# Attention inside a fused kernel: value sums for two batches in one product, the next x transposed ahead of the head products, and the key product in a bank of its own

## The reference

```python
q, k, v = split_heads(layernorm(x) @ w_qkv.T)
dots = q @ k.T                                  # per head, no softmax
attn = dots / max(norm(dots), EPS) * norm_g + norm_b
x = x + layernorm(merge_heads(attn @ v) @ w_out.T + b_out)
x = x + layernorm(soft_moe(layernorm(x)))       # 8 experts, 128 slots each
```

## Time and profile before

| what | value |
|---|---|
| median of 3 runs | 839.48 us |
| the three runs | 839.48, 839.47, 840.86 us |
| the profiled execution, its own time | 840.9 us |
| its span, first to last instruction | 839.1 us |
| mean granted TensorE clock | 0.998 |
| TensorE busy | 831.7 us, 99% |
| VectorE busy | 643.9 us, 77% |
| ScalarE busy | 549.1 us, 65% |

### The profile page before, as it was taken

The page is one execution under the profiler, slowest core; times in us unless marked ns, Lnnn a source line. Parts: engine busy times, 40 slices in busy tenths (PEclk is TensorE's granted clock), DMA queues, the critical chain, the costliest instruction groups (busy, mean ns, idle before and its releaser), DMA issues.

```text
span 839.1 us, 15012 instructions
## 1 busy us (share of the span) xinstructions
PE 831.7 (99%) x4890; PEld 723.0 (86%) x4890; DVE 643.9 (77%) x1296; ACT 549.1 (65%) x1078; POOL 86.3 (10%) x103
## 2 busy tenths in 40 slices
PE   9999999999999999999999999999999999999997
PEld 8988999887888888888988888888888888899997
DVE  8788888899899989998866666666666665477776
ACT  5666767567787887789546555555555554567775
POOL 0200000043223333450000000000000000000000
PEclk9999999999999999999999999999999999999999
DMA  7011121202323252125020303011020303066883
GB/s 246 21 51 51 50 75 39 63 26 77 106 97 124 89 201 98 67 96 207 1 100 1 101 1 100 0 65 35 16 84 0 100 0 101 1 203 215 286 289 112
DMA packets 52561, 75.37 MB, mean 90 GB/s; under 512 B 3104, under 2 KB 33696, under 8 KB 52384
## 3 DMA queue, kind: packets, MB, share of 16 engines
q1 hardware_dynamic: 52512, 74.76, 26.8%
HBM read 49.59 MB, written 25.17 MB: 89 GB/s over the span
## 4 chain that ended last, share of the span: by engine, by line
PE 93%; DVE 4%; ACT 1%; issue 1%; DMA 0%; DVEq 0%; POOL 0%; ACTq 0%; POOLq 0%
PE bank L996 21%; PE bank L1026 13%; PE bank L1068 11%; PE bank L865 9%; PE bank L890 9%; PE bank L1029 7%; PE bank L785 3%; PE bank L874 3%; PE bank L735 3%; PE bank L684 2%; PE bank L768 2%; PE bank L758 1%; PE bank L746 1%; PE bank L1004 1%; PE bank L716 1%; PE bank L705 1%
## 5 line engine op out<-in xcount | busy, mean ns | idle before, releaser
L996 PE MATMUL bank<-snT,w_r 128*128 128x512 f32 x768 | 194.8, 393 | 0.0
L1471 ACT ACTIVATE act<-bank,b_sb 128x512 f32<-128x512 f32 x128 | 88.0, 687 | 139.3 <-PE bank L996 138.9
L2085 DVE TENSOR_TENSOR act_r<-act,act_r 128x512 fp32r<-128x512 f32 x128 | 88.2, 690 | 111.0 <-ACT act_r L1476 110.8
L1026 PE MATMUL bank<-w_r,act_r 128*128 128x512 f32 x480 | 173.2, 397 | 0.0
L996 PEld LDWEIGHTS bank<-snT,w_r 128*128 128x128 f32 x768 | 136.6, 188 | 28.7 <-issue 0.3
L1029 PE MATMUL bank<-w_r,act_r 128*128 128x256 f32 x480 | 134.6, 280 | 0.0
L1026 PEld LDWEIGHTS bank<-w_r,act_r 128*128 128x128 f32 x480 | 90.2, 188 | 21.0
L890 PE MATMUL bank<-disp_r,y_r 128*128 128x512 f32 x384 | 103.5, 406 | 0.4 <-DVE disp_r L1938 0.3
L865 PE MATMUL bank<-yT_r,snT 128*128 128x512 f32 x384 | 99.4, 395 | 0.0
L1029 PEld LDWEIGHTS bank<-w_r,act_r 128*128 128x128 f32 x480 | 90.7, 189 | 4.1
L1068 PE MATMUL bank<-eo_r,comb_r 128*128 128x258 f32 x768 | 92.3, 283 | 0.0
(11 more groups left out here) (203 smaller groups left out, 1321.3 us busy)
## 6 DMA issues: line engine op xcount, KB each, us to landing
combine_scratch<-comb SPq DMA_DIRECT2D x64, 256.0 KB, 2.0
stage<-in_w SPq DMA_DIRECT2D x16, 1024.0 KB, 6.5
stage<-combine_scratch SPq DMA_DIRECT2D x4, 2048.0 KB, 9.1
snT<-combine_scratch SPq DMA_DIRECT2D x4, 2048.0 KB, 9.5
x_scratch<-stage SPq DMA_DIRECT2D x8, 512.0 KB, 3.2
x<-x_scratch SPq DMA_DIRECT2D x8, 512.0 KB, 4.0
x_d<-x_scratch SPq DMA_DIRECT2D x8, 512.0 KB, 9.6
slots_eo<-in_x SPq DMA_DIRECT2D x7, 512.0 KB, 4.4
```

Of the source, the lines that this page charges most:

```text
L996: last = pe.matmul(hidden_bank(e, i)[:, :], w1_r[q][:, a, k, j * P:(j + 1) * P], sl_r[f][:, c, k, :], start=(n == 0), stop=(n == len(steps ...
L1026: pe.matmul(bank[BH + c][:, :].rearrange("p (w d) -> p w d", w=2), act_r[:, i % RING, 0, c * S:(c + 1) * S], w2_r[q][:, :, j, :], start=(j ...
L1471: act_fn(act[:, i % 2, :], hidden_bank(e, i)[:, :], ACT.Gelu, bias=b1_sb[:, ds(e * KH + i % KH, 1)])\
L2085: v.tensor_tensor(act_r[:, i % RING, 1, :], act[:, i % 2, :], act_r[:, i % RING, 0, :].bitcast(F32), ALU.subtract).then_inc(h_split, 1)
```

## The change

- `value_sums` is issued in batches 0 and 1 for one batch each, and then in each odd batch for that batch and the one before. `xsum` has two rows for this, and the product has two columns. It stands behind the queries (in batch 0 it stays where it was), and goes into bank 0. VectorE's product with b_col moves out of `keep_heads` into `keep_sums`, which stands ahead of `rest_of_gk` in odd batches, with a semaphore `vb_kept`.
- `transpose_xn(b + 1)` stands between `transpose_o(b-1)` and `head_products(b)`. ScalarE's and VectorE's work on it (`round_xnT`, `rest_of_xnT`) moves from the start of the next batch to the end of this one, on VectorE ahead of `keep_proj`, and after batches 1 and 2 ahead of the slots.
- The key product goes into bank 3 and waits for VectorE's clamp of the norms there.
- The loop runs over pairs of batches.

```diff
-            xsum = sb("xsum", [P, KD])
+            xsum = sb("xsum", [P, 2, KD])
...
+        def sums_through(b, odd, it):
+
+            if isinstance(b, int):
+                return b + 1 if b < 2 else 2 + (b - 1) // 2
+            return it + 3
...
-                    pe.wait_ge(gk_split, b)
+                    pe.wait_ge(qT_ready, b * KD)
+                    if not odd:
+                        pe.wait_ge(vb_kept, sums_through(b - 1, True, it))
...
-                pe.wait_ge(qT_ready, b * KD + 1)
+                if not is_batch(b, 0):
+                    pe.wait_ge(norm_clamped, b)
...
-                        last = pe.matmul(bank[0][:, m * D:(m + 1) * D], gram_r[:, i, k, m * P:(m + 1) * P],
+                        last = pe.matmul(bank[3][:, m * D:(m + 1) * D], gram_r[:, i, k, m * P:(m + 1) * P],
...
             def value_sums(b):
+
+                pair = slice(b, b + 1) if is_batch(b, 0) or is_batch(b, 1) else slice(0, 2)
+                pe.wait_ge(qT_ready, b * KD + 1)
                 for h in range(KD):
                     for k in range(KD):
-                        last = pe.matmul(bank[3][:, h:h + 1],
-                                         wqkvT[:, k, 2 * D + h * P:2 * D + (h + 1) * P], xsum[:, k:k + 1],
+                        last = pe.matmul(bank[0][:, 2 * h + pair.start:2 * h + pair.stop],
+                                         wqkvT[:, k, 2 * D + h * P:2 * D + (h + 1) * P], xsum[:, pair, k],
...
-                if front:
-                    queries(b)
-                if front:
-                    gram_times_k(b)
+                queries(b)
+                if odd:
+                    value_sums(b)
+                gram_times_k(b)
                 if back:
                     transpose_o(b - 1)
-                if front:
+                if not back:
                     value_sums(b)
-                    if not back:
-                        half_of_xn(1)
-                    head_products(b)
+                    half_of_xn(1)
+                elif not before_y:
+                    transpose_xn(b + 1, False, not odd, it)
+                head_products(b)
...
-            with pe.Fori(3, B - 1) as b:
-                attention(b)
+            with pe.Fori(0, B // 2 - 2) as it:
+                attention(2 * it + 3, True, it)
+                attention(2 * it + 4, False, it)
...
                 if following and back:
                     round_xn(b + 1)
+                    round_xnT(b + 1, not odd, it)
...
-                dve.wait_ge(sums_in_psum, b + 1)
-                v.tensor_tensor(vb[:, ds(b % 2, 1), :].rearrange("p a c -> p (a c)"), bank[3][:, 0:KD], b_col[:],
-                                ALU.mult).then_inc(heads_ready, 1)
+                last.then_inc(heads_ready, 1)
+
+            def keep_sums(b, it=0):
+
+                pair = slice(b, b + 1) if is_batch(b, 0) or is_batch(b, 1) else slice(0, 2)
+                n = pair.stop - pair.start
+                dve.wait_ge(sums_in_psum, sums_through(b, True, it))
+                v.tensor_tensor(vb[:, pair, :], bank[0][:, 0:2 * KD].rearrange("p (h a) -> p a h", a=2)[:, pair, :],
+                                b_col[:].unsqueeze(1).to_broadcast([P, n, KD]), ALU.mult).then_inc(vb_kept, 1)
...
+                if odd:
+                    keep_sums(b, it)
                 if front:
                     rest_of_gk(b)
...
                 if following and back:
                     rest_of_xn(b + 1)
+                    rest_of_xnT(b + 1)
```

More of the change, by code:

```diff
@@ L798, in transpose_slots, with attention @@
                     last.then_inc(seT_in_psum, 1)
-            def attention(b, front=True, back=True, first_back=False, second_back=False, before_y=False):
-                if front:
+            def attention(b, odd, it=0, back=True, first_back=False, second_back=False, before_y=False):
+                if is_batch(b, 0) or is_batch(b, 1):
                     transpose_xn(b, not back)
-                    gram_of_x(b, not back)
+                gram_of_x(b, not back)
                 if back:
@@ L1143, in round_second, with round_xnT @@
                 act_fn(xn_r[:, 0, half:NT], xn[:, half:NT], ACT.Copy).then_inc(xn_hi, 1)
-            def round_xnT(b, first):
-                if not first:
+            def round_xnT(b, odd, it=0):
+                if not is_batch(b, 0):
                     sc.wait_ge(qT_in_psum, b * KD)
-                    sc.wait_ge(sums_in_psum, b)
+                if isinstance(b, int) and b >= 2:
+                    sc.wait_ge(sums_in_psum, sums_through(b - 2 if b < 4 else b - 1, True, 0))
+                elif not isinstance(b, int):
+                    sc.wait_ge(sums_in_psum, it + 3)
                 for k in range(KD):
@@ L1174, in round_gk @@
                 sc.wait_ge(gk_in_psum, b + 1)
-                act_fn(gk_r[:, 0], bank[0][:, :].rearrange("p (k d) -> p k d", k=KD), ACT.Copy).then_inc(gk_hi, 1)
+                act_fn(gk_r[:, 0], bank[3][:, :].rearrange("p (k d) -> p k d", k=KD), ACT.Copy).then_inc(gk_hi, 1)
             def keep_qT(b, h, first):
@@ L1186, in root_norm, with round_oT @@
                 act_fn(nrm[:], nrm[:], ACT.Sqrt, bias=zero_col[:]).then_inc(norm_rooted, 1)
-            def round_oT(b, first):
+            def round_oT(b, first, odd, it=0):
                 if not first:
                     sc.wait_ge(proj_in_psum, b)
+                sc.wait_ge(vb_kept, sums_through(b + 1 if not odd and not first else b, True, it))
                 for h in range(KD):
@@ L1194, in round_oT @@
                     alone(sc)
-                    act_fn(oT_r[:, 0, h, :], bank[4 + h][:, :], ACT.Identity, bias=vb[:, ds(b % 2, 1), h:h + 1]
-                           .rearrange("p a c -> p (a c)")).then_inc(oT_hi, 1)
+                    act_fn(oT_r[:, 0, h, :], bank[4 + h][:, :], ACT.Identity, bias=vb[:, int(odd), h:h + 1])\
+                        .then_inc(oT_hi, 1)
             def square_proj(b, first=False, begin=0, end=NT):
@@ L1241, in mean_out_bias, with attention @@
                     .then_inc(bout_summed, 1)
-            def attention(b, front=True, following=True, back=True, end=True, first_back=False, first_end=False,
-                          before_y=False):
+            def attention(b, odd, it=0, front=True, following=True, back=True, end=True, first_back=False,
+                          first_end=False, before_y=False):
                 if before_y:
                     root_x2(0, B // 2)
-                if front:
-                    round_xnT(b, not back)
+                if is_batch(b, 0) or is_batch(b, 1):
+                    round_xnT(b, odd)
                 if front and not back:
@@ L1287, in attention @@
                 if back:
-                    round_oT(b - 1, first_back)
+                    round_oT(b - 1, first_back, not odd, it)
                 if before_y:
@@ L1835, in attention @@
                 if back:
-                    rest_of_oT(b - 1)
+                    rest_of_oT(b - 1, not odd)
                 if first_back:
@@ L1841, in attention @@
                     dve.wait_ge(consts_loaded, 16 * N_CONSTS)
+                if not back:
+                    keep_sums(b)
                 if front:
@@ L1884, in _ @@
             rest_of_wqkv(0)
[L1885 to L1886 removed]
+            attention(0, False, back=False, end=False)
+            attention(1, True, end=False, first_back=True)
             rest_of_slots(0)
[L1888 removed]
+            attention(2, False, first_end=True)
             rest_of_slots(1)
[L1890 to L1892 removed]
+            with dve.Fori(0, B // 2 - 2) as it:
+                attention(2 * it + 3, True, it)
+                attention(2 * it + 4, False, it)
+            attention(B - 1, True, following=False, before_y=True)
             dve.wait_ge(ident_loaded, 16)
```

49 lines of the change are left out of this document (23 added, 26 removed).

## The result

The changed kernel takes 836.80 us (median of 6 runs, 836.57 to 836.92), against 839.49 for the kernel before (6 runs: 839.47, 839.47, 839.48, 839.50, 840.86, 841.01). The ratio of the means is 0.9962, with a 95% interval of 0.9949 to 0.9975. That is 0.3 to 0.4% faster, clear of the noise. Between the medians it is 2.7 us, where 2.1 was forecast. The runs of before fall into two groups, a lower one at 839.5 and an upper one at 840.9 and 841.0, the runs with a stretch at half clock. In these six runs the changed kernel shows no second group.

A forecast was written before the change was run, and what follows sets the result against it. TensorE, busy 99% at full clock, was taken as the bound. Sums -2.43, batch 3's wait -0.40 and batch 7's lost cover +0.75 make -2.08 us, from the median 839.48 to 837.4 us; range 836.7 to 838.0.

The forecast's parts named there:

- The value sums are work: TensorE's value sums: 0.81 us a group is work, not a hidden wait; three groups fewer give -2.43 us.
- The second column is free: Value sums for two batches in one product: the second column was taken as zero cost, 0.3 us in all at most.
- The lost cover in batch 7: Batch 7 has nothing between o transposes and head products, so TensorE waits for gk_r: +0.75 us.
- The moved transposes: xn transposes (0.79) replace value sums (0.81) ahead of the head products; cover 1.66 instead of 1.68 still suffices for gk_r.
- The Gram and the transposes show no wait: After the move xn is 0.28 us early for the transposes and xn_r 0.58 early for the Gram: no wait.
- The gain is carried through: After the attention no TensorE wait over 0.3 us is on the chain, so the gain reaches the end; contrary rival 0.08.
- The wait in batch 3: TensorE's 0.42 us wait for qGq ahead of batch 3's norm products shrinks, 0.02 to 0.2 left: -0.40 us.
- No row there has a wait: Batch 4 of the loop, read by starts on TensorE: its groups' times were taken to hold no wait.
- Batch 3, the one place where TensorE waits: Claimed batch 3, after outputs, as TensorE's only wait: 0.42 us for VectorE's qGq.
- The half clock: Batch 3's queries at 1.2 GHz behind a wait and narrow norm products cost 1.58 us; rival that it stays, 0.14.
- The rival that batch 7's new wait would bring it: Batch 7's new 0.75 wait, or the one left in batch 3, brings half clock in most runs: 839.0, chance 0.14.
- slower: the clock falls again and again: Narrow sums close behind norm products drop the clock in batches 1, 3, 5, 7: 6.3 us, 843.7; chance 0.04.

The follow-up runs named there:

- `slots_first`: The changed kernel with VectorE's rest of xnT of batch 3 behind the last slots again; 838.03 and 838.08 us in two runs, 839.20 to 839.71 in eight, 841.05 in one.
- `slots_unrolled`: `slots_first` with TensorE's batches 3 to 6 written out; 838.03 and 838.07 us in two runs, 839.41 to 839.68 in nine.
- `before_pairs`: The kernel before with ScalarE and VectorE looping over pairs of batches, so the column of vb is a constant; 838.88 us.
- `vb_by_batch`: The changed kernel with a column of vb for every batch, its address worked out in a register in the loop; 837.88 us.
- `sums_ahead`: The changed kernel with the value sums of batches 1, 3, 5, 7 ahead of the norm products; 839.75 to 839.81 us in three runs, 840.98 to 841.47 in eight.
- `slots_filled`: `slots_unrolled` with five unused 512-column products ahead of batch 3's norm products, where TensorE waits for qGq; 837.98 to 838.14 us in six runs.
- `own_sums`: The changed kernel with one-column value sums for each batch, behind the queries, so three groups more; 839.56 us.

## Why the prediction was right or wrong

**Right, by its own steps.** The value sums are work, 0.81 a group: term -2.43, measured -2.39. The second column is free: 0.80 and 0.81 a group in batches 5 and 7, and 0.80 with one column in batch 1. The group of batch 3 takes 0.91; in `slots_first` and `slots_unrolled`, where TensorE comes to it later, it takes 0.81, so the extra 0.1 is most likely a wait, which no run tests by itself. The lost cover in batch 7: +0.75, measured +0.76, and shown by filling it. The moved transposes keep the head products supplied: no wait for gk_r in batches 1 to 6, and 5.5 us lost when they are moved back, 4.6 of it as this wait. The Gram and the transposes show no wait from batch 4 on; in batch 3 a new one of about 0.2 stands between the Gram and gram times q, which the forecast did not have. The gain is carried through. The wait in batch 3: -0.40 forecast; the outputs lost 0.51 and the norm products' restart 0.01 there, but 0.12 and 0.09 came back as the new wait ahead of gram times q, and 0.1 at the value sums; about -0.2 net.

**Wrong: a wait was taken for work.** The step that failed is the reading of batch 4 by starts, with its end "No row there has a wait". Head products 1.56 and projection 2.94 in the earlier trace rows were taken for plain work, so the sum has nothing for them. They hold a wait of TensorE for VectorE's oT_r, and the runs show 0.66 us for its going. The Gram that was to start 2.94 after the projection starts 2.80 after it. The written-out batch 2 of the kernel before has these rows, which I did not use:

```profile
53.69 1.68 PE L716 MATMUL bank<-wqkv_r,gk_r 128*128 128x256 f32 x12
55.20 2.97 PE L785 MATMUL bank<-wout_r,oT_r 128*128 128x256 f32 x24
58.01 1.03 PE L796 MATMUL bank<-ident,slots_eo 128*128 128x128 f32 x8
```

1.51 and 2.81 for the same instructions. The loop's projections waited for oT_r, in which `vb[:, ds(b % 2, 1)]` had its address worked out in a register on both engines. The loop over pairs turned it into a constant. In batches 3 to 6 the head products and projections give 0.66 us less, which `before_pairs` confirms as 0.6 in the time. That the address is what made oT_r late is shown in two batches of `vb_by_batch`, 0.15 us each; for the whole 0.66 it is the likely cause and not shown. I had listed the loop over pairs as part of the change and given it no price.

**A second term, small in sum.** A group of rounded products takes 0.08 more behind full-precision ones: Gram 1.99 behind transposes and 1.92 behind the projection, key product 1.52 behind sums and 1.44 behind queries. The move saves it at four Grams and, in the same size, at two groups of slot transposes, which now have rounded products behind them (0.87 to 0.79), and pays it at four key products: -0.32 - 0.16 + 0.32 = -0.16.

**A third.** "Batch 3, the one place where TensorE waits" isn't so: in batch 2 of the kernel before the norm products start 0.06 after VectorE's qGq is done (44.64 + 1.25 = 45.89, and 45.95). Outputs, norm products and queries take 1.85 + 1.81 + 2.81 = 6.47 there and 1.79 + 1.70 + 2.85 = 6.34 after the change: -0.13.

With all three the sum is -2.08 - 0.66 - 0.16 - 0.13 = -3.03, and with +0.2 for batch 3 it is -2.83. Measured are -2.69 between the medians and -2.84 in the traces. The missed terms are -0.95 and +0.2, so they cancel in part.

**The clock.** The half clock was read rightly as following the wait and the narrow products ahead of the queries, and 1.58 as its price. Median against median it does not count, as forecast. The rival that batch 7's new wait would bring it has no execution for it. The rival "slower: the clock falls again and again" did not happen in the changed kernel, but `sums_ahead` shows that it is real: there the same sums stand beside the norm products and not behind the 2.85 us of queries, and the clock falls in batches 1, 3 and 7. The Trainium skill (TensorE: Matmul & The Clock Gate, What's actually happening) says that the clock is set by how busy TensorE has been. The trace agrees in `slots_filled`, where work in the wait keeps the granted clock at 1.00. In batch 3 of `sums_ahead` TensorE is busy all the time ahead of the queries, a pass every 0.11 us, and the granted clock in them is 0.52 all the same; there the measurement decides.

**Open:** the slower pace of the projections in `vb_by_batch` (some 0.5 us) and another 0.3 there, and 0.03 a group in `own_sums`.

## What to carry to other kernels

Compare the same group in a loop and where it is written out: a tenth of a microsecond more in the loop can be a wait that no view lists. When work is taken from between a producer and its consumer, ask what else covers the way through the other engines, and put work there that must be done anyway. Keep groups of very narrow products apart, with wide ones between them: side by side they cost this kernel 4.5 us at the median through TensorE's clock.

## What the runs showed of the hardware

- Behind 2.7 us of back-to-back products of one to eight columns, without any wait, TensorE's granted clock was 0.50 to 0.52 in the wide products, in three of four batches of `sums_ahead`: 4.3 to 4.4 us for queries that take 2.85.
- With a register address in the operand of ScalarE's and VectorE's oT_r operations, VectorE's started 0.2 us later (0.86 against 0.66 between starts, batches 4 and 6 of `vb_by_batch`; 0.89 against 0.60 to 0.65 in batches 3 to 6, the kernel before against `before_pairs`, whose loops differ too). In batches 3 and 5 of `vb_by_batch` it did not.
- A group of rounded products took 0.08 us more behind full-precision ones than behind rounded ones (Gram 1.99 and 1.92, key product 1.52 and 1.44). Moving the sums in `sums_ahead` took the 0.08 from the key product, and the norm products took 0.08 more instead. A full-precision group is 0.08 shorter from start to start when rounded products follow it (0.79 against 0.87 for transposes), so the runs don't show that the change costs time in sum.
